# Windowed attention on 64 image passes: TensorE's round in another order, the output in a score bank, the normalised images held twice

## The chip, the cores and the metric

The kernel runs on one core of a Trainium2 chip. The metric is the device time of one execution in microseconds. Three runs of the kernel before took 764.14, 768.58 and 770.73 us, so the median is 768.58.

## What is computed

Two layers, each a group normalisation and a shifted-window attention with a residual, on 32 images of 16 x 16 tokens and 256 channels:

```python
x = x + _L0_conv_ref(_gn(x), ...)
x = x + _L1_conv_ref(_gn(x), ...)
# one layer, on windows of 64 tokens, 16 heads of 16 channels:
q, k, v = xw @ Wq.T, xw @ Wk.T, xw @ Wv.T + bv
qn, kn = q / norm(q), k / norm(k)
logits = einsum(qn, kn) * exp(min(logit_scale, LOG100)) + 16 * sigmoid(bias)
scores = softmax(where(mask, -inf, logits))
z = (scores @ v) @ Wo.T + bo
```

`_gn` takes mean and variance over a group of 8 channels and all tokens of an image.

## The kernel before

All images stay in SBUF (`x_all`). A **job** is one image in one layer; there are 64. Each engine runs the same function `iteration(j, base)` for rounds j = -3 to 67, unrolled at the ends and in loops of two rounds in between. In round j four jobs are in flight: `now` is job j, `before` j-1, `older` j-2 and `oldest` j-3; normalising works ahead for jobs j+1 to j+3. The order of the work on an engine is the order of the calls in its `iteration`, written out by hand; every engine goes through it strictly in that order, and they meet on semaphores.

TensorE, round j: the group sums of job j+2 (L433), q and k of `now` into both banks of `ps_qk` (L380, two halves of 6 matmuls), turning back the mixed values of `oldest` (L392), turning q and k of `before` into score banks 0 and 1 (L404), the output projection of `oldest` (L414 for the rounded part, L419 for the rest), the scores of `before` (L469), the mixing of `older`, that is probabilities times values (L486, L496), and v of `now` (L508). Matmuls with the weights take two parts of the operand, a rounded one and the rest, three products in all. The output projection writes `ps_mix` bank 0, as the mixing does; the mixing therefore waits until the residual of `oldest` has been added.

ScalarE: squares of q/k (L574), rounding the next normalised image (`round_xn`, L581), the rounded mixed values (L588), q masked by head (`keep_q`, L596), logarithm and exponential that seed the inverse roots (L609, L618), the exponential of the scores in two halves (L643), normalising job j+2 into the one buffer `xn32` (L626), and v (L651).

VectorE: group variance of job j+2 (four small operations, L803 to L809), moments of job j+3 (`moments`, L750), norm sums (L758, twice), the rest of the mixed values (L775), k (L767), residual (L794, twice), unit vectors of q/k (`make_unit`, L783, twice), and the division of the mixed values by their sums (`divide`, L816 to L823).

GpSimd: squares of the moments of job j+3 (`mean_squares`, L927 to L933), the rest of the next normalised image (`split_xn`, L919), Newton's step for the inverse roots (`newton`, L943 to L956), and the weighing of the probabilities of `before` with the bias (`weigh`, L963, four times).

So q/k of job j+1 in round j+1 waits for `split_xn` of round j (semaphore `xn_ready`), the unit vectors wait for `newton`, the mixing for the four weighings of the round before, the division for the mixing (`mix_done`), and `mean_squares` for `moments` (`bn_done`). A second pass with exact maxima stands behind a test at the end; it isn't taken with this input.

Of the kernel before, what the change touches and what calls it, by code (L numbers as in the profile page):

```python
# [83 lines left out]
def build(nc, x, weights, out, consts, table_scratch):  # L84
    with ExitStack() as ctx:
# [46 lines left out]
        xn32 = sb("xn32", [P, CC, TOKENS])  # L132
# [35 lines left out]
        z_cols = ps_mix[:, 0, :].rearrange("p (c t) -> p c t", c=CC)  # L168
# [177 lines left out]
        def _(pe):  # L346
# [60 lines left out]
            def project_out(t):  # L407
                if t is None:
                    return
                pe.wait_ge(mixed_hi, t.count(1, 1))  # L410
                for c in range(CC):
                    for a in range(2):
                        for part in range(2):
                            nc.tensor.matmul(z_cols[:, c, :], w_o[:, part, a, c * P:(c + 1) * P], mixed[:, 0, a, :],  # L414
                                             start=(c + a + part == 0), stop=False, skip_group_check=True)
                pe.wait_ge(mixed_ready, t.count(1, 1))
                for c in range(CC):
                    for a in range(2):
                        last = nc.tensor.matmul(z_cols[:, c, :], w_o[:, 0, a, c * P:(c + 1) * P], mixed[:, 1, a, :],  # L419
                                                start=False, stop=(a == 1), skip_group_check=True)  # L420
                last.then_inc(z_done, 1)
# [33 lines left out]
            def score(j, base, t):  # L455
# [5 lines left out]
                past(pe, exped, t.count(2, 0))  # L461
                refine(t)
# [14 lines left out]
            def mix(j, base, t):  # L477

                if t is None:
                    return  # L480
                past(pe, x_updated, t.count(2, 0))
                past(pe, mixed_ready, t.count(1, 0))
                pe.wait_ge(v_ready, t.count(1, 1))
                pe.wait_ge(weighted, t.count(4, 4))

                nc.tensor.matmul(mix_cols[:, 0, 0, :], probs[0:N, t.parity, 0, 0, 0, :, :].rearrange("p a n -> p (a n)"),  # L486
                                 v_ones[0:N, t.parity, 0, 0, 0, 0, :], start=True, stop=True, skip_group_check=True)
                for e in range(2):
                    for c in range(CC):
                        for r in range(GROUPS):  # L490
                            for a in range(2):
                                for w in range(2):
                                    if e + c + r + a + w == 0:
                                        continue
                                    at = slice(w * N, (w + 1) * N)
                                    last = nc.tensor.matmul(mix_cols[a * N:(a + 1) * N, w, (e * CC + c) * GROUPS + r, :], probs[at, t.parity, r, e, c, a, :],  # L496
                                                            v_ones[at, t.parity, e, c, r, a, :], start=True, stop=True, skip_group_check=True)
                last.then_inc(mix_done, 1)
# [13 lines left out]
            def iteration(j, base):  # L512
# [8 lines left out]
                sum_groups(j, base, job(j, base, 2))  # L521
                project_qk(now, 0)
                project_qk(now, 1)
                turn_back(oldest)
                turn(before)
                project_out(oldest)
                score(j, base, before)
# [6 lines left out]
                mix(j, base, older)  # L534
                if j == 0:
                    pe.wait_ge(w_split, split(0, base.exact, 1))
# [9 lines left out]
        def _(act):  # L546
# [29 lines left out]
            def round_xn(t):  # L576
# [4 lines left out]
                nc.scalar.activation(xn[:, 0, t.parity, :, :], xn32[:, :, :], ACT.Copy).then_inc(xn_hi, 1)  # L581
# [38 lines left out]
            def normalise(u):  # L620
# [3 lines left out]
                past(act, xn_ready, u.count(1, 0))  # L624
                for c in range(CC):
                    nc.scalar.activation(xn32[:, c, :], x_all[:, bass.ds(u.image, 1), c, :].rearrange("p o t -> p (o t)"), ACT.Identity,  # L626
# [27 lines left out]
            def iteration(j, base):  # L654
# [7 lines left out]
                round_xn(job(j, base, 1))  # L662
                square(now, 1)
                keep_mixed(oldest)
                keep_q(before, 0)
                keep_q(before, 1)
# [6 lines left out]

# [6 lines left out]
                if j == IMAGES + 2:  # L680
                    act.wait_ge(z_done, oldest.count(1, 1))
                    round_weights(1, 2)
                keep_shift(before)
                for i in range(GROUPS // 2):
                    exp(before, i)
                normalise(job(j, base, 2))
                keep_v(now)
                if j == -1:
                    round_weights(0, 1)
# [11 lines left out]
        def _(dve):  # L701
# [148 lines left out]
            def iteration(j, base):  # L850
# [5 lines left out]
                group_variance(j, base, after)  # L856
                moments(ahead)
# [9 lines left out]
                sum_norms(base, now, 0)  # L867
                sum_norms(base, now, 1)
# [6 lines left out]
                refine_shift(before)  # L875
                cap(before)
# [8 lines left out]
                divide(older)  # L885
                if j == 0 and not base.exact:
# [21 lines left out]
        def _(pool):  # L908
# [6 lines left out]
            def split_xn(t):  # L915
# [3 lines left out]
                nc.gpsimd.tensor_tensor(xn[:, 1, t.parity, :, :], xn32[:, :, :], xn[:, 0, t.parity, :, :], ALU.subtract).then_inc(xn_ready, 1)  # L919
# [45 lines left out]
            def iteration(j, base):  # L965
                if j >= 0:
                    mean_squares(job(j, base, WARM))
                split_xn(job(j, base, 1))
                newton(j, base)
                if j < 0:  # L970
                    mean_squares(job(j, base, WARM))
# [86 lines left out]
```

## Time and profile before

| | |
|---|---|
| runs, median | 768.58 us (764.14 to 770.73) |
| span of the profiled execution | 768.5 us; no time of its own is listed beside it |
| TensorE busy | 728.5 us, 95% |
| TensorE weight loads | 652.5 us, 85% |
| VectorE busy | 503.5 us, 66% |
| ScalarE busy | 498.5 us, 65% |
| GpSimd busy | 553.6 us, 72% |
| chain that ended last | TensorE 89% |
| DMA | in the first 80 us, then 19 to 32 GB/s for the stores and late loads |

The busy shares are means over the span. In a kernel with one loop the rows of the loop tell more: the timeline shows when each engine starts what, and in brackets how long it had been idle and who ended that. The chain of waits shows each piece of the path that ended last, with the time that it holds.

### The profile page before, as it was taken

To read this page: it belongs to the slowest core of one execution; us is meant where nothing else is said; L and a number is where in the kernel's file an instruction comes from. 1 tells how busy PE (TensorE), PEld (TensorE's weight loads), DVE (VectorE), ACT (ScalarE), POOL (GpSimd) and SP (SyncE) were. 2 spreads that over 40 slices of the span, in tenths; PEclk is the share of its full clock that TensorE was granted. 3 is DMA by queue.
4 is the path that set the end of the run, shared out by engine and by line. 5 is a ranking of instruction groups with operands and counts; after the bars stand their busy time and mean duration, and the time that the engine had idled before them with its cause. 6 is when DMAs were issued, how large, how long until landed. Compare 5 with 4: busy or idle time off the path is not lost.

```text
span 768.5 us, 38488 instructions
## 1 busy us (share of the span) xinstructions
PE 728.5 (95%) x15518; PEld 652.5 (85%) x15518; DVE 503.5 (66%) x1177; ACT 498.5 (65%) x848; POOL 553.6 (72%) x913
## 2 busy tenths in 40 slices
PE   3689899999999999999999999999999999999995
PEld 3578788888888889898989888888888888888984
DVE  4545466666666666667777667677766767776642
ACT  4556467676677667676777676666667666666650
POOL 4475668777877787788888777877777787777660
PEclk9789899999999999999999999999999999999995
DMA  4666200000000000000000000000000000000000
GB/s 116 156 157 172 65 0 0 0 1 0 0 0 0 0 0 0 0 0 0 1 0 0 28 28 14 27 27 25 16 27 27 14 27 27 27 14 27 29 31 32
DMA packets 14041, 21.45 MB, mean 28 GB/s; under 512 B 3756, under 2 KB 5045, under 8 KB 14005
## 3 DMA queue, kind: packets, MB, share of 16 engines
q1 hardware_dynamic: 13461, 20.23, 8.8%
q10 hardware_dynamic: 544, 0.79, 0.3%
q8 instruction: 17, 0.28, 0.2%
q14 instruction: 19, 0.16, 0.1%
HBM read 12.60 MB, written 8.42 MB: 27 GB/s over the span
## 4 chain that ended last, share of the span: by engine, by line
PE 89%; issue 3%; DVE 3%; DMA 2%; DVEq 1%; ACT 0%; SPq 0%; ACTq 0%
PE ps_qk L380 24%; PE ps_mix L496 17%; PE ps_qk L508 14%; PE ps_mix L414 9%; PE ps_score L404 7%; PE ps_score L469 6%; PE ps_mix L419 4%; PE ps_mix L392 4%; PE ps_mix L486 3%; DVE x_out L794 2%; DMA bias_rev<-table_scratch 1%; PE ps_score L433 1%; DMA table_scratch<-table 1%; DMA cpb<-in_L_cpb 0%; DVE exp_bias L737 0%
## 5 line engine op out<-in xcount | busy, mean ns | idle before, releaser
L963 POOL TENSOR_TENSOR probs<-probs,exp_bias 128x512 f32<-128x512 f32 x256 | 326.0, 1305 | 18.9 <-ACT probs L643 18.9
L380 PE MATMUL ps_qk<-w_qk,xn 128*128 128x512 f32 x768 | 200.0, 410 | 0.0
L643 ACT ACTIVATE probs<-ps_score,lower 128x1024 f32<-128x1024 f32 x128 | 135.7, 1111 | 66.8 <-PE ps_score L469 66.8
L380 PEld LDWEIGHTS ps_qk<-w_qk,xn 128*128 128x128 f32 x768 | 144.0, 194 | 30.2
L496 PE MATMUL ps_mix<-v_ones,probs 64*64 64x17 f32 x8064 | 133.4, 209 | 3.4 <-issue 3.4
L574 ACT ACTIVATE squares<-ps_qk 128x512 f32<-128x512 f32 x128 | 77.0, 602 | 87.1 <-PE ps_qk L380 87.1
L758 DVE TENSOR_REDUCE sums_sq<-squares 128x32 f32<-128x512 f32 x128 | 87.2, 682 | 68.9 <-ACT squares L574 68.8
L496 PEld LDWEIGHTS ps_mix<-v_ones,probs 64*64 64x64 f32 x8064 | 126.8, 136 | 5.5 <-issue 3.7
L783 DVE SCALAR_TENSOR_TENSOR unit<-root,ps_qk 128x512 f32<-128x512 f32 x128 | 82.4, 683 | 58.9 <-POOL root L953 58.9
L508 PE MATMUL ps_qk<-w_v,xn 128*128 128x256 f32 x768 | 113.9, 300 | 5.4 <-DVE unit L783 4.6
L508 PEld LDWEIGHTS ps_qk<-w_v,xn 128*128 128x128 f32 x768 | 100.2, 198 | 7.7 <-issue 6.0
L943 POOL TENSOR_TENSOR refined<-sums_sq,seed 128x66 f32<-128x66 f32 (+2 forms) x66 | 21.3, 322 | 97.6 <-ACT seed L618 97.5
L651 ACT ACTIVATE v_ones<-ps_qk 128x512 f32<-128x512 f32 x64 | 38.4, 601 | 77.4 <-PE ps_qk L508 77.4
L919 POOL TENSOR_TENSOR xn<-xn 128x512 fp32r<-128x512 f32 x64 | 82.0, 1281 | 5.5 <-ACT xn L581 5.5
L596 ACT ACTIVATE q_own<-ps_score,own_head 128x512 f32<-128x512 f32 x128 | 81.1, 693 | 0.0
L414 PE MATMUL ps_mix<-mixed,w_o 128*128 128x256 f32 x512 | 78.5, 296 | 1.4 <-ACT mixed L588 1.4
L469 PE MATMUL ps_score<-q_own,k_rows 32*64 32x128 f32 x4096 | 77.2, 278 | 2.4 <-DVE k_rows L767 1.2
L414 PEld LDWEIGHTS ps_mix<-mixed,w_o 128*128 128x128 f32 x512 | 65.0, 190 | 9.1 <-ACT mixed L588 2.0
L626 ACT ACTIVATE xn<-x_all,g_off,root 128x256 f32 (+1 forms) x128 | 69.5, 596 | 3.3 <-POOL g_off L956 3.3
L469 PEld LDWEIGHTS ps_score<-q_own,k_rows 32*64 32x64 f32 x4096 | 61.8, 130 | 11.2 <-ACT q_own L596 2.8
L404 PE MATMUL ps_score<-ident,unit 128*128 128x128 f32 x512 | 66.3, 273 | 0.0
L404 PEld LDWEIGHTS ps_score<-ident,unit 128*128 128x128 f32 x512 | 58.0, 140 | 0.3
(73 smaller groups left out, 867.8 us busy)
## 6 DMA issues: line engine op xcount, KB each, us to landing
x_all<-in_x SPq DMA_DIRECT2D x32, 256.0 KB, 3.1
out<-x_out SPq DMA_DIRECT2D x32, 256.0 KB, 2.1
bias_rev<-table_scratch SPq DMA_DIRECT2D x4, 452.0 KB
w_qk_in<-in_L_matrices ACTq DMA_DIRECT2D x1, 512.0 KB, 4.6
w_o_in<-in_L_matrices SPq DMA_DIRECT2D x4, 128.0 KB
w_qk_in<-in_L_matrices SPq DMA_DIRECT2D x1, 512.0 KB, 5.5
w_v_in<-in_L_matrices ACTq DMA_DIRECT2D x1, 256.0 KB, 4.9
w_v_in<-in_L_matrices SPq DMA_DIRECT2D x1, 256.0 KB, 6.2
```

Source lines behind the costliest of these rows:

```text
L380: last = nc.tensor.matmul(ps_qk[:, e, :], xn[:, px, t.parity, c, e * P:(e + 1) * P], w_qk[:, pw, c, :], start=(c == 0 and i == 0), stop=(c ...
L404: last = nc.tensor.transpose(to[:, e, c, :], unit[:, e, (n * CC + c) * P:(n * CC + c + 1) * P], ident[:, :])
L414: nc.tensor.matmul(z_cols[:, c, :], w_o[:, part, a, c * P:(c + 1) * P], mixed[:, 0, a, :], start=(c + a + part == 0), stop=False, skip_gro ...
L469: last = nc.tensor.matmul(ps_score[w * N:(w + 1) * N, r, cols:cols + 2 * N], k_rows[at, e, c, w * N:(w + 1) * N], q_own[at, e, c, w, :, :] ...
L496: last = nc.tensor.matmul(mix_cols[a * N:(a + 1) * N, w, (e * CC + c) * GROUPS + r, :], probs[at, t.parity, r, e, c, a, :], v_ones[at, t.p ...
L508: last = nc.tensor.matmul(v_cols[:, e, :], xn[:, px, t.parity, c, e * P:(e + 1) * P], w_v[:, pw, c, :], start=(c == 0 and i == 0), stop=(c ...
L596: nc.scalar.activation(q_own[:, :, :, :, a, :].rearrange("p e c w n -> p (e c w) n"), q_turned_to.rearrange("p e c (w n) -> p (e c w) n", ...
L643: nc.scalar.activation(probs[:, t.parity, 2 * i:2 * i + 2, :, :, :, :].rearrange("p r e c a n -> p r (e c a n)"), ps_score[:, 2 * i:2 * i ...
L758: nc.vector.tensor_reduce(sums_sq[:, e * NORMS:(e + 1) * NORMS], squares[:, e, :].rearrange("p (h d) -> p h d", d=HD), AX_X, ALU.add).then ...
L783: nc.vector.scalar_tensor_tensor(out=unit[:, e, :].rearrange("p (h d) -> p h d", d=HD), in0=by, scalar=INV_NORM_TOP, in1=ps_qk[:, e, :].re ...
L919: nc.gpsimd.tensor_tensor(xn[:, 1, t.parity, :, :], xn32[:, :, :], xn[:, 0, t.parity, :, :], ALU.subtract).then_inc(xn_ready, 1)
L963: nc.gpsimd.tensor_tensor(pr, pr, exp_bias[:, t.layer, r, :, :, :, :].rearrange("p e c a n -> p (e c a n)"), ALU.mult).then_inc(weighted, 1)
```

## The change

On TensorE the group sums go behind q/k, the scores behind the mixing, and the output projection writes score bank 3 in place of the mixing's bank 0. It waits for the exponentials of job j-2 before it writes there; the waits of the mixing (v and the weighings) now stand in the middle of the output projection, and the scores wait for the residual. The mixing's first double-width matmul goes. `xn32` is held twice, by parity. ScalarE rounds and normalises ahead of the exponentials, does logarithm and seed ahead of q, and keeps v between the two exponentials. On VectorE the group variance goes between the two norm sums and the moments behind the division. On GpSimd Newton's step and the squares of the moments come first, then the split.

```diff
-        xn32 = sb("xn32", [P, CC, TOKENS])
+        xn32 = sb("xn32", [P, 2, CC, TOKENS])
...
-        z_cols = ps_mix[:, 0, :].rearrange("p (c t) -> p c t", c=CC)
+        z_cols = ps_score[:, 3, :].rearrange("p (c t) -> p c t", c=CC)
...
+            def await_mix(t):
+                pe.wait_ge(v_ready, t.count(1, 1))
+                pe.wait_ge(weighted, t.count(4, 4))
+
+            def project_out(t, older):
                 if t is None:
                     return
+                if older is not None:
+                    pe.wait_ge(exped, older.count(2, 2))
                 pe.wait_ge(mixed_hi, t.count(1, 1))
...
                 pe.wait_ge(mixed_ready, t.count(1, 1))
+                if older is not None:
+                    await_mix(older)
...
                 past(pe, exped, t.count(2, 0))
+                oldest = job(j, base, -3)
+                if oldest is not None:
+                    pe.wait_ge(x_updated, oldest.count(2, 2))
                 refine(t)
...
-                past(pe, x_updated, t.count(2, 0))
-                past(pe, mixed_ready, t.count(1, 0))
-                pe.wait_ge(v_ready, t.count(1, 1))
-                pe.wait_ge(weighted, t.count(4, 4))
-
-                nc.tensor.matmul(mix_cols[:, 0, 0, :], probs[0:N, t.parity, 0, 0, 0, :, :].rearrange("p a n -> p (a n)"),
-                                 v_ones[0:N, t.parity, 0, 0, 0, 0, :], start=True, stop=True, skip_group_check=True)
+                if job(j, base, -3) is None:
+                    await_mix(t)
...
-                                    if e + c + r + a + w == 0:
-                                        continue
...
-                sum_groups(j, base, job(j, base, 2))
                 project_qk(now, 0)
                 project_qk(now, 1)
+                sum_groups(j, base, job(j, base, 2))
                 turn_back(oldest)
                 turn(before)
-                project_out(oldest)
-                score(j, base, before)
+                project_out(oldest, older)
...
                 mix(j, base, older)
+                score(j, base, before)
...
-                past(act, xn_ready, u.count(1, 0))
+                past(act, xn_ready, u.count(1, -1))
                 for c in range(CC):
-                    nc.scalar.activation(xn32[:, c, :], x_all[:, bass.ds(u.image, 1), c, :].rearrange("p o t -> p (o t)"), ACT.Identity,
+                    nc.scalar.activation(xn32[:, u.parity, c, :], x_all[:, bass.ds(u.image, 1), c, :].rearrange("p o t -> p (o t)"), ACT.Identity,
...
                 square(now, 0)
-                round_xn(job(j, base, 1))
                 square(now, 1)
                 keep_mixed(oldest)
-                keep_q(before, 0)
-                keep_q(before, 1)
...
+                keep_q(before, 0)
+                keep_q(before, 1)
+                round_xn(job(j, base, 1))
+                normalise(job(j, base, 2))
                 keep_shift(before)
-                for i in range(GROUPS // 2):
-                    exp(before, i)
-                normalise(job(j, base, 2))
+                exp(before, 0)
                 keep_v(now)
+                exp(before, 1)
...
-                group_variance(j, base, after)
-                moments(ahead)
+                if j < 0:
+                    group_variance(j, base, after)
+                    moments(ahead)
...
                 sum_norms(base, now, 0)
+                if j >= 0:
+                    group_variance(j, base, after)
                 sum_norms(base, now, 1)
...
                 make_unit(base, now, 0)
                 divide(older)
+                if j >= 0:
+                    moments(ahead)
...
             def iteration(j, base):
-                if j >= 0:
-                    mean_squares(job(j, base, WARM))
+                newton(j, base)
+                mean_squares(job(j, base, WARM))
                 split_xn(job(j, base, 1))
-                newton(j, base)
-                if j < 0:
-                    mean_squares(job(j, base, WARM))
```

TensorE, round 3 as it was (names are the destination and the operands):

```order
L433 MATMUL ps_score<-bn_sum,consts 128x4
L380 MATMUL ps_qk<-w_qk,xn 128x512 x12
L392 MATMUL ps_mix<-ident,o_rows 128x2x64 x4
L404 MATMUL ps_score<-ident,unit 128x128 x8
L414 MATMUL ps_mix<-mixed,w_o 128x256 x8
L419 MATMUL ps_mix<-mixed,w_o 128x256 x4
L469 MATMUL ps_score<-q_own,k_rows 64x128 x32
L486 MATMUL ps_mix<-v_ones,probs 128x17
L496 MATMUL ps_mix<-v_ones,probs 64x17 x63
L508 MATMUL ps_qk<-w_v,xn 128x256 x12
```

And the same round of the change:

```order
L380 MATMUL ps_qk<-w_qk,xn 128x512 x12
L441 MATMUL ps_score<-bn_sum,consts 128x4
L392 MATMUL ps_mix<-ident,o_rows 128x2x64 x4
L404 MATMUL ps_score<-ident,unit 128x128 x8
L420 MATMUL ps_score<-mixed,w_o 128x256 x8
L427 MATMUL ps_score<-mixed,w_o 128x256 x4
L500 MATMUL ps_mix<-v_ones,probs 64x17 x64
L480 MATMUL ps_score<-q_own,k_rows 64x128 x32
L512 MATMUL ps_qk<-w_v,xn 128x256 x12
```

The scores stand behind the mixing, and the output's destination is `ps_score`.

VectorE at the end of a round in the loop, before, with what each row waits for: division, then the next round's group variance.

```order
L816 TENSOR_SCALAR sums<-ps_mix 128x32 [waits mix_done]
L209 ISA
L818 TENSOR_TENSOR least<-least,ps_mix 128x32 [waits sum_step]
L819 REGISTER_ALU
L820 RECIPROCAL inv_sums<-sums 128x32 [waits sum_step]
L821 REGISTER_ALU
L823 TENSOR_TENSOR o_rows<-ps_mix,inv_sums 128x512 [waits turned_back,sum_step]
L801 REGISTER_ALU
L803 TENSOR_SCALAR neg_mean<-ps_score 128x2 [waits gn_offset,group_summed]
```

The same place in the change:

```order
L819 TENSOR_SCALAR sums<-ps_mix 128x32 [waits mix_done]
L209 ISA
L821 TENSOR_TENSOR least<-least,ps_mix 128x32 [waits sum_step]
L822 REGISTER_ALU
L823 RECIPROCAL inv_sums<-sums 128x32 [waits sum_step]
L824 REGISTER_ALU
L826 TENSOR_TENSOR o_rows<-ps_mix,inv_sums 128x512 [waits turned_back,sum_step]
L748 ISA
L753 ISA [waits moment_step,x_moved1]
L753 BN_STATS bn<-x_all 128x6
```

The moments (`BN_STATS`) now follow the division, whose first row waits for the mixing of the same round.

GpSimd at the start of a round in the loop, before: squares, split, then Newton's step.

```order
L927 TENSOR_TENSOR mean_sq<-bn 128x4 [waits bn_done]
L928 TENSOR_SCALAR bn<-bn 128x4
L929 ISA
L930 TENSOR_TENSOR bn<-bn,mean_sq 128x4 [waits moment_step]
L931 REGISTER_ALU
L209 REGISTER_ALU [waits moment_step]
L933 TENSOR_TENSOR bn_sum<-bn 128x4 [waits group_summed]
L918 ISA
L919 TENSOR_TENSOR xn<-xn 128x512 [waits xn_hi]
L942 REGISTER_ALU
L943 TENSOR_TENSOR refined<-sums_sq,seed 128x66 [waits seeded]
```

And in the change, from the last row of Newton's step on:

```order
L964 TENSOR_TENSOR g_off<-root,neg_mean 128x2 [waits newton_step]
L934 REGISTER_ALU
L935 TENSOR_TENSOR mean_sq<-bn 128x4 [waits bn_done]
L936 TENSOR_SCALAR bn<-bn 128x4
L937 ISA
L938 TENSOR_TENSOR bn<-bn,mean_sq 128x4 [waits moment_step]
L939 REGISTER_ALU
L209 REGISTER_ALU [waits moment_step]
L941 TENSOR_TENSOR bn_sum<-bn 128x4 [waits group_summed]
L926 REGISTER_ALU
L927 TENSOR_TENSOR xn<-xn 128x512 [waits xn_hi]
```

The split (`xn<-xn`) stands directly behind the squares in both; the squares have moved behind Newton's step, and what they wait for, `bn_done`, now comes from the end of VectorE's round.

## Rows read from the trace of the kernel before

**Rows 1.** Busy time by stretches: us, busy (instructions) per engine, granted clock, DMA share, GB/s

```profile
300.00:400.00 100.00, 99.69 (x2185) 89.41 (x2184) 74.19 (x170) 70.93 (x121) 81.89 (x127) 1.00 0.00 0
```

**Rows 2.** Timeline of TensorE, starts of q/k: start, us, what

```profile
16.94 4.53 PE L380 MATMUL ps_qk<-w_qk,xn 128*128 128x512 f32 x12
...
107.84 2.35 PE L380 MATMUL ps_qk<-w_qk,xn 128*128 128x512 f32 x9
...
729.73 2.95 PE L380 MATMUL ps_qk<-w_qk,xn 128*128 128x512 f32 x12
```

**Rows 3.** Chain of waits, one round: start, us held, what

```profile
406.71 2.90 PE ps_qk L380 x12
...
412.46 1.14 PE ps_score L469 x63
...
413.60 0.39 PE ps_mix L486 x2
...
415.97 1.62 PE ps_qk L508 x12
```

**Rows 4.** Waits in total: us, times, longest

```profile
PEld ps_mix L486 <- issue: 20.0, 59, 0.5
...
PE ps_mix L486 <- DVE x_out L794: 3.9, 13, 1.0
```

**Rows 5.** Timeline of a steady round, all engines

```profile
405.03 0.19 DVE L816 TENSOR_SCALAR sums<-ps_mix 128x32 f32<-128x32 f32 x1 [0.52 <-PE ps_mix L496]
...
405.64 0.69 DVE L823 TENSOR_TENSOR o_rows<-ps_mix,inv_sums 128x512 f32<-128x512 f32 x1
...
406.43 0.28 PE L433 MATMUL ps_score<-bn_sum,consts 128*128 128x4 f32 x2
...
406.56 3.04 PE L380 MATMUL ps_qk<-w_qk,xn 128*128 128x512 f32 x12
...
406.74 0.16 DVE L803 TENSOR_SCALAR neg_mean<-ps_score 128x2 f32<-128x2 f32 x1 [0.41 <-PE ps_score L433]
...
407.68 0.74 DVE L750 BATCH_NORM_STATS2 bn<-x_all 128x6 f32<-128x256 f32 x2
...
409.64 0.60 ACT L574 ACTIVATE squares<-ps_qk 128x512 f32<-128x512 f32 x1 [0.28 <-PE ps_qk L380]
```

**Rows 6.** Timeline of the first rounds, VectorE and GpSimd

```profile
4.10 0.75 DVE L750 BATCH_NORM_STATS2 bn<-x_all 128x6 f32<-128x256 f32 x2 [4.10 <-DMA x_all<-in_x]
...
4.93 0.20 POOL L927 TENSOR_TENSOR mean_sq<-bn 128x4 f32<-128x4 f32 x1 [2.77 <-DVE bn L750]
...
22.13 0.69 DVE L758 TENSOR_REDUCE sums_sq<-squares 128x32 f32<-128x512 f32 x1 [0.94 <-ACT squares L574]
...
25.23 1.28 DVE L783 SCALAR_TENSOR_TENSOR unit<-root,ps_qk 128x512 f32<-128x512 f32 x2 [2.41 <-POOL root L953]
```

**Rows 7.** Timeline of GpSimd in a steady round

```profile
182.62 5.03 POOL L963 TENSOR_TENSOR probs<-probs,exp_bias 128x512 f32<-128x512 f32 x4 [0.20 <-ACT probs L643]
...
187.61 0.20 POOL L927 TENSOR_TENSOR mean_sq<-bn 128x4 f32<-128x4 f32 x1
...
188.59 1.27 POOL L919 TENSOR_TENSOR xn<-xn 128x512 fp32r<-128x512 f32 x1
```

**Rows 8.** Timeline of TensorE in early rounds, with its idle time before

```profile
51.74 0.54 PE L496 MATMUL ps_mix<-v_ones,probs 64*64 64x17 f32 x25 [0.98 <-issue]
...
64.03 0.42 PE L496 MATMUL ps_mix<-v_ones,probs 64*64 64x17 f32 x14 [1.04 <-issue]
...
64.37 2.77 PE L508 MATMUL ps_qk<-w_v,xn 128*128 128x256 f32 x12
...
92.43 2.50 PE L508 MATMUL ps_qk<-w_v,xn 128*128 128x256 f32 x10 [0.76 <-issue]
...
95.01 4.72 PE L380 MATMUL ps_qk<-w_qk,xn 128*128 128x512 f32 x12
```

**Rows 9.** Busy time by stretches, an early one

```profile
65.00:70.00 5.00, 5.00 (x24) 4.50 (x23) 2.17 (x8) 1.25 (x3) 2.75 (x6) 0.70 0.60 161
```

More of the change, by code:

```diff
@@ L405, in turn @@
                     last.then_inc(done, 1)
-            def project_out(t):
+            def await_mix(t):
+                pe.wait_ge(v_ready, t.count(1, 1))
+                pe.wait_ge(weighted, t.count(4, 4))
+            def project_out(t, older):
                 if t is None:
                     return
+                if older is not None:
+                    pe.wait_ge(exped, older.count(2, 2))
                 pe.wait_ge(mixed_hi, t.count(1, 1))
@@ L580, in round_xn @@
                 past(act, v_done, t.count(1, -1))
-                nc.scalar.activation(xn[:, 0, t.parity, :, :], xn32[:, :, :], ACT.Copy).then_inc(xn_hi, 1)
+                nc.scalar.activation(xn[:, 0, t.parity, :, :], xn32[:, t.parity, :, :], ACT.Copy).then_inc(xn_hi, 1)
             def keep_mixed(t):
@@ L874, in iteration @@
                 add_residual(oldest, 1)
-                refine_shift(before)
-                cap(before)
                 if j == IMAGES:
@@ L885, in iteration @@
                 divide(older)
+                if j >= 0:
+                    moments(ahead)
+                refine_shift(before)
+                cap(before)
                 if j == 0 and not base.exact:
@@ L918, in split_xn @@
                 pool.wait_ge(xn_hi, t.count(1, 1))
-                nc.gpsimd.tensor_tensor(xn[:, 1, t.parity, :, :], xn32[:, :, :], xn[:, 0, t.parity, :, :], ALU.subtract).then_inc(xn_ready, 1)
+                nc.gpsimd.tensor_tensor(xn[:, 1, t.parity, :, :], xn32[:, t.parity, :, :], xn[:, 0, t.parity, :, :], ALU.subtract).then_inc(xn_ready, 1)
             def mean_squares(u):
```

## The prediction

> **What bounds the kernel now.** I read the busy time by stretches first. In the middle of the run TensorE is busy for 99.7 of 100 us at the full granted clock of 1.00 (2.4 GHz), the other three engines for 71 to 82 [rows 1]. So the loop is TensorE's own work, and there is no stall in it to take away beyond splinters. The timeline of TensorE gives the length of a round, from one start of the q/k projection to the next: 107.84 to 729.73 us for 56 rounds, 11.1 us each. The first seven rounds, 16.94 to 107.84, took 90.9 us, 13.0 each [rows 2]. The chain of waits shows one round as TensorE spends it [rows 3]. The splinters are in front of the mixing: its first weight load waits for the issue of its waits, 20.0 us in 59 rounds, and for the residual that still reads the mixing's bank, 3.9 us in 13 [rows 4]. Those are what TensorE itself can win.
>
> The question is then whether the other engines' new order still lets TensorE run without a stall. For that I follow everything that a round must finish before the next q/k projection may start.
>
> **The change on TensorE.** The output goes into bank 3 of the scores, so the mixing no longer waits for the residual, and its waits are issued ahead of the last four output matmuls, behind work that is in the queue. The first double-width matmul of the mixing, 0.39 us with its stall, becomes two of the small ones, of which the other 126 records fill 413.99 to 415.97, 1.98 us [rows 3]: 0.03. Taken with [rows 4] this is at best 24 us over the run, 0.35 to 0.4 us a round. The score now waits for the residual and for q and k, but the mixing (2.0 us) lies between the turning and it, so I cost these waits at nothing; without that cover the score would stall by the residual's 0.9 us. The group sums behind q/k cost their 0.12 us in either place.
>
> **The change on VectorE and GpSimd.** Here is the step that decides. Before, the moments of the image three ahead are taken at the start of VectorE's round, beside the q/k projection, and GpSimd squares them right after the weighing of the round before. Now VectorE takes them **behind the division**, which is the last thing that it does in a round, and GpSimd, which is in order, has their squares **ahead of the split of the next image**. The next q/k projection waits for that split. So the end of each round now hangs on the division. The cycle, counted from the start of q/k in round j:
>
> - q/k takes 2.90 us on TensorE [rows 3], then come the group sums. VectorE starts the group variance 0.31 us after they do (406.43 to 406.74) and needs 0.94 us for it (406.74 to 407.68) [rows 5]: 2.90 + 0.31 + 0.94 = 4.15 us. The second half's squares are there by 3.1 + 0.6 = 3.7 us (409.64 against 406.56, the start of that q/k) [rows 5], so the second norm sum now starts at 4.15, 0.4 later than its data allow.
> - From the start of that sum to the start of the unit vectors, through the logarithm, the seed and Newton's four steps, a round in which nothing else stood in between took 25.23 - 22.13 = 3.10 us [rows 6]: 7.25. In today's steady rounds ScalarE copies q between sum and logarithm; the change moves that behind the seed, so I take the clean round. The two unit products take 1.28 [rows 6]: 8.53.
> - The mixing is through at 415.97 - 406.71 - 1.14 (the score, now behind it) + 0.13 (the sums, now ahead) - 0.36 (the first matmul) = 7.9 us. The unit vectors are the later of the two releases by 0.6.
> - The division takes 405.03 to 406.33, 1.30 us [rows 5]: 9.83. The moments take 0.75 and reach GpSimd 0.08 us after their end (4.85 to 4.93) [rows 6]: 10.66. Squares and sums take 187.61 to 188.59, 0.98, and the split 1.27 [rows 7]: 12.91. For the hop from GpSimd to TensorE I take 0.1, the size of the one that the rows show.
>
> The cycle is **13.0 us**, against the 10.75 of TensorE's work. It replaces the 11.1 us of today: +1.9 us a round. Are the other cycles shorter? With the mixing in place of the unit vectors it is 12.4. Through the weighing (5.03 us [rows 7]): hop 0.1, last output 0.5, mixing 2.0, division 1.3, moments and hop 0.83, squares 0.98, split 1.27, weighing 5.03, 12.0 us. Both give way. GpSimd ends the weighing 5.0 us after q/k starts, when the seed comes at about 5.6, so it isn't late for Newton. The second copy of the normalised images frees ScalarE from waiting for the split, and costs nothing; normalising has more than 2 us ahead of the exponential.
>
> How many rounds: the moments exist up to round 60, so the start of q/k is held back up to round 61. From round 7 to 61 that is 54 intervals, 54 x 1.9 = 103 us. The first seven rounds are as long as the new cycle already; some of their stalls are TensorE's instruction issue in the mixing, which is 0.6 us off the cycle, so I add 3 us (0 to 10). The last rounds gain under 1. With the clock untouched: 768.5 + 103 + 3 = **874 us**. The span of the profiled execution, 768.5, lies on the median of the runs, 768.58, so no correction.
>
> **The clock.** With a round of 13.0 and 10.75 of work, TensorE stands idle for about 2.3 us in each round, between v and q/k. No steady round has such a gap now, and what the clock does after one must be read at the start of the run. There TensorE stood still for 0.98 us at 50.8, for 1.04 at 63.0 and for 0.76 at 91.7. After the first nothing happened; after the second v took 2.77 us in place of 1.62 and the granted clock of 65 to 70 us was 0.70 [rows 9]; after the third ten of the twelve matmuls of v took 2.50 and q/k 4.72 in place of 2.90 [rows 8]. That is the lower level, 1.2 GHz, over one or two products. So two of three shorter gaps than the new one brought a fall, 1.1 us of it where it lay on v and 1.8 on q/k. The new gap is right ahead of q/k, which is the head of the cycle, so a fall is paid in full. But dense products stand on both sides of it, where the mixing's small matmuls stood beside the old ones, so I take half of the 57 rounds held back, at 1.6 us: 57 x 0.5 x 1.6 = 46 us. Bounds: none, and 1.8 in all 57, 103 us.
>
> The Trainium skill (TensorE: Matmul & The Clock Gate, section "Why this matters for your kernels") warns of throughput drops only for idle gaps that are longer than this one. By it the clock would stay up and the time would be 874 us; the early rounds here speak against it, with falls after 1.04 and 0.76 us.
>
> Sum: 874 + 46 = **920 us**.
>
> **The rivals.**
> - *The clock stays at 2.4 GHz*: the cycle of 13.0 alone, 874 us. For it: the fall that did not come after 0.98 us, and the dense products on both sides. Against: the gap is twice as long as those that brought a fall. 0.26.
> - *Faster, TensorE stays the bound*: if a round's moments didn't hold back the split, the cycle would end at the weighing and be under 10.75, and TensorE would win its splinters: 768.5 - 24 = 745 us. It decides at a cycle of 10.75 us, 2.25 below my sum. Each term has its own row, and the order of VectorE and GpSimd is fixed by the program, so for this the hops or the overlaps would have to be misread by 2 us. 0.04.
> - *The cycle is real but shorter*, 11.5 to 12.5 us, because the steps overlap more than their rows show: 785 to 850 us. 0.04.
> - *The clock falls in nearly every round*, or for longer than q/k, so that turning and output are slow too: 960 to 1000 us. 0.06.
> - *Nothing moves*: the wait sits on GpSimd, which is idle for a fifth of the time, and TensorE doesn't feel it. It would need a split that is a round early, which the order excludes. 0.02.
>
> My forecast has 0.58. One per cent, some 8 us, is about what a measurement of this kernel can tell from no change. Faster 0.04, within 1% 0.02, slower 0.94. The range takes in the case with the clock up, less a little for a cycle of 12.8 us, and ends where the falls come in nine rounds of ten: 864 to 958.
>
> **What would show it.** GpSimd's squares of the moments wait for VectorE's moments some 3 us in each of about 60 rounds, near 190 us, where its largest wait on that pair is now small. TensorE's first q/k matmul waits for GpSimd's split, 2 us or more in each round, over 100 us in all, in a place that has no wait now. The start of q/k comes every 13.0 us in rounds without a fall, and the mixing's first matmul has no issue gap left. VectorE has the group variance between its two norm sums. TensorE's busy share falls below 86%, and the granted clock shows slices below 9 through the whole loop; if these stay at 9, the first rival holds. Starts of q/k every 10.8 us would prove the whole sum wrong; the first place to look would then be GpSimd's queue, whether the split waits behind the squares at all.

## The result and the profile after

The changed kernel takes **949.08 us** (948.28 to 956.52) against 769.12 for the kernel before, measured beside each other: a ratio of 1.237 [1.230, 1.244]. The prediction was 920 us, in a range of 864 to 958. Time and sign are right; two of its terms are off, one by 51 us and one by 35, in opposite directions, and the experiments are mostly about these. Two executions that have no trace stand out: the one of 956.52 us shows a mean granted clock of 0.741, where the other three of the changed kernel have 0.946 to 0.950, and one of experiment 8 took 1784.54 us, about twice its others, for a reason that is not known, and is left out there.

The page of the changed kernel: busy time, the granted clock in 40 slices, and the chain that ended last by engine and by line.

```profile
PE 756.3 (80%) x15518; PEld 658.4 (69%) x15518; DVE 509.7 (54%) x1177; ACT 517.6 (55%) x848; POOL 552.4 (58%) x913
...
PEclk9789999899899999998989999899999999999995
...
POOL 42%; issue 34%; PE 10%; DMA 4%; DVE 4%; POOLq 2%; SPq 2%; ACT 1%; DVEq 0%
...
POOL probs L971 26%; PE ps_qk L380 4%; DMA x_all<-in_x 4%; POOL xn L927 4%; POOL refined L955 2%; POOL refined L953 2%; POOL refined L951 2%; POOL root L961 2%; POOL mean_sq L935 2%; POOL bn L938 1%; PE ps_mix L500 1%; POOL bn L936 1%; POOL g_off L964 1%; PE ps_score L427 1%; PE ps_score L420 1%
```

TensorE's share went from 95% to 80%. The clock has slices below 9 in the loop, where it was 1.00 [rows 1], but few. The chain now names GpSimd first, its weighing above all. That line is a trap, as the fourth experiment shows.

The starts of q/k on TensorE, to be read against [rows 2]:

```profile
17.28 5.46 PE L380 MATMUL ps_qk<-w_qk,xn 128*128 128x512 f32 x12 [6.20 <-POOL xn L927]
...
116.39 3.05 PE L380 MATMUL ps_qk<-w_qk,xn 128*128 128x512 f32 x12 [2.27 <-POOL xn L927]
...
881.42 3.05 PE L380 MATMUL ps_qk<-w_qk,xn 128*128 128x512 f32 x12 [1.65 <-POOL xn L927]
...
903.39 2.96 PE L380 MATMUL ps_qk<-w_qk,xn 128*128 128x512 f32 x12
```

From round 7 to round 61 it is 881.42 - 116.39 = 765.0 us, 14.17 a round, where the kernel before took 600.4, 11.12. That is 164.6 of the 179.1 us by which the span grew (947.6 against 768.5). The first seven rounds give 8.5, the last ones 6. In the last ones the output projection waits for the weighings, with nothing else to do; two such waits are in the timeline, 2.6 us together, and the other 3.4 are not split up here:

```profile
918.80 0.71 PE L427 MATMUL ps_score<-mixed,w_o 128*128 128x256 f32 x4 [1.08 <-POOL probs L971]
...
931.16 1.19 PE L427 MATMUL ps_score<-mixed,w_o 128*128 128x256 f32 x4 [1.49 <-POOL probs L971]
```

One steady round of the changed kernel, all engines, with the idle time in brackets:

```profile
144.11 5.01 POOL L971 TENSOR_TENSOR probs<-probs,exp_bias 128x512 f32<-128x512 f32 x4
...
144.28 3.05 PE L380 MATMUL ps_qk<-w_qk,xn 128*128 128x512 f32 x12 [2.24 <-POOL xn L927]
...
147.49 0.16 DVE L806 TENSOR_SCALAR neg_mean<-ps_score 128x2 f32<-128x2 f32 x1 [0.20 <-PE ps_score L441]
...
148.07 1.08 DVE L812 TENSOR_SCALAR sums_sq<-g_var 128x2 f32<-128x2 f32 x1
...
149.06 0.68 DVE L761 TENSOR_REDUCE sums_sq<-squares 128x32 f32<-128x512 f32 x1
...
152.53 1.29 DVE L786 SCALAR_TENSOR_TENSOR unit<-root,ps_qk 128x512 f32<-128x512 f32 x2 [0.30 <-POOL root L961]
...
153.73 0.18 DVE L819 TENSOR_SCALAR sums<-ps_mix 128x32 f32<-128x32 f32 x1
...
154.94 0.74 DVE L753 BATCH_NORM_STATS2 bn<-x_all 128x6 f32 x2
...
155.76 0.20 POOL L935 TENSOR_TENSOR mean_sq<-bn 128x4 f32<-128x4 f32 x1 [3.00 <-DVE bn L753]
...
156.76 1.26 POOL L927 TENSOR_TENSOR xn<-xn 128x512 fp32r<-128x512 f32 x1
...
157.98 1.29 POOL L971 TENSOR_TENSOR probs<-probs,exp_bias 128x512 f32<-128x512 f32 x1
```

Read it from 144.28. The variance (L806) starts 3.21 us later, as reckoned from [rows 5]. Its last step (L812) takes 1.08 us, and ends as the fourth weighing of the block of 144.11 ends (144.11 + 5.01 = 149.12). The second norm sum starts at 4.78, the units (L786) at 8.25, the division at 9.45, the moments at 10.66, GpSimd's squares (L935) at 11.48, the split at 12.48, and q/k of the next round with the next block at about 13.88. The waits in total:

```profile
POOL mean_sq L935 <- DVE bn L753: 187.7, 62, 4.1
...
PE ps_qk L380 <- POOL xn L927: 136.6, 61, 6.2
...
PE ps_score L427 <- DVE mixed L778: 23.4, 41, 0.7
```

The first two are what the prediction said would be seen, 188 us and 137 us. The third is new.

### The profile page after: what moved, and what is told of

Read it like the earlier page. It is cut to its first block, busy times and chain, and to the rows that moved or that the text cites. A ratio compares the mean times of both kernels' runs of the same rounds, so it can differ in the third digit from the quotient of the medians.

```text
span 947.6 us, 38578 instructions
## 1 busy us (share of the span) xinstructions
PE 756.3 (80%) x15518; PEld 658.4 (69%) x15518; DVE 509.7 (54%) x1177; ACT 517.6 (55%) x848; POOL 552.4 (58%) x913
## 4 chain that ended last, share of the span: by engine, by line
POOL 42%; issue 34%; PE 10%; DMA 4%; DVE 4%; POOLq 2%; SPq 2%; ACT 1%; DVEq 0%
POOL probs L971 26%; PE ps_qk L380 4%; DMA x_all<-in_x 4%; POOL xn L927 4%; POOL refined L955 2%; POOL refined L953 2%; POOL refined L951 2%; POOL root L961 2%; POOL mean_sq L935 2%; POOL bn L938 1%; PE ps_mix L500 1%; POOL bn L936 1%; POOL g_off L964 1%; PE ps_score L427 1%; PE ps_score L420 1%
## 5 line engine op out<-in xcount | busy, mean ns | idle before, releaser
L380 PE MATMUL ps_qk<-w_qk,xn 128*128 128x512 f32 x768 | 226.6, 451 | 138.7 <-POOL xn L927 136.6
L971 POOL TENSOR_TENSOR probs<-probs,exp_bias 128x512 f32<-128x512 f32 x256 | 321.0, 1286 | 15.0 <-ACT probs L647 15.0
L380 PEld LDWEIGHTS ps_qk<-w_qk,xn 128*128 128x128 f32 x768 | 160.8, 216 | 187.2 <-issue 145.6
L647 ACT ACTIVATE probs<-ps_score,lower 128x1024 f32<-128x1024 f32 x128 | 142.3, 1113 | 40.9 <-PE ps_score L480 40.9
L935 POOL TENSOR_TENSOR mean_sq<-bn 128x4 f32<-128x4 f32 x64 | 16.5, 257 | 187.7 <-DVE bn L753 187.7
L512 PE MATMUL ps_qk<-w_v,xn 128*128 128x256 f32 x768 | 109.4, 292 | 5.6 <-DVE unit L786 4.6
L512 PEld LDWEIGHTS ps_qk<-w_v,xn 128*128 128x128 f32 x768 | 96.1, 191 | 16.6 <-issue 16.4
L786 DVE SCALAR_TENSOR_TENSOR unit<-root,ps_qk 128x512 f32<-128x512 f32 x128 | 82.4, 684 | 18.4 <-POOL root L961 18.1
L420 PE MATMUL ps_score<-mixed,w_o 128*128 128x256 f32 x512 | 77.8, 295 | 3.7 <-ACT mixed L592 3.7
L420 PEld LDWEIGHTS ps_score<-mixed,w_o 128*128 128x128 f32 x512 | 66.1, 192 | 13.7 <-issue 5.0
L427 PE MATMUL ps_score<-mixed,w_o 128*128 128x256 f32 x256 | 46.0, 303 | 25.9 <-DVE mixed L778 23.4
```

What stands on the lines that cost most here:

```text
L380: last = nc.tensor.matmul(ps_qk[:, e, :], xn[:, px, t.parity, c, e * P:(e + 1) * P], w_qk[:, pw, c, :], start=(c == 0 and i == 0), stop=(c ...
L512: last = nc.tensor.matmul(v_cols[:, e, :], xn[:, px, t.parity, c, e * P:(e + 1) * P], w_v[:, pw, c, :], start=(c == 0 and i == 0), stop=(c ...
L647: nc.scalar.activation(probs[:, t.parity, 2 * i:2 * i + 2, :, :, :, :].rearrange("p r e c a n -> p r (e c a n)"), ps_score[:, 2 * i:2 * i ...
L786: nc.vector.scalar_tensor_tensor(out=unit[:, e, :].rearrange("p (h d) -> p h d", d=HD), in0=by, scalar=INV_NORM_TOP, in1=ps_qk[:, e, :].re ...
L971: nc.gpsimd.tensor_tensor(pr, pr, exp_bias[:, t.layer, r, :, :, :, :].rearrange("p e c a n -> p (e c a n)"), ALU.mult).then_inc(weighted, 1)
```

## The experiments

Each was timed beside the kernel before, which took 768.3 to 770.7 us in these comparisons.

**1. Moments back at the start of VectorE's round**, all else as changed.

```diff
                 if j < 0:
                     group_variance(j, base, after)
-                    moments(ahead)
+                moments(ahead)
...
                 divide(older)
-                if j >= 0:
-                    moments(ahead)
```

> The changed kernel, with the moments of job j+3 back at the start of VectorE's round; all else as changed. Theory 1 (the moments behind the division close a cycle of 14.0 us over weighing, variance, norm sum, Newton, units, division, moments, squares and split): the cycle is cut, what is left is GpSimd's own loop, weighing 5.0 + norm sum to the end of Newton 3.8 + squares 1.0 + split 1.26 = 11.1 us a round, or TensorE's 10.75: 750 to 775 us. Rival (the loss lies in TensorE's new order and the waits in the middle of the output projection): the time stays over 900 us.

Measured: 793.39 us, ratio 1.032 [1.028, 1.035]. One call in another place takes away 156 of the 180 us. Rounds take 11.5 us. TensorE is the bound but for one stall, which is in the timeline of this kernel:

```profile
312.42 0.63 PE L392 MATMUL ps_mix<-ident,o_rows 128*128 128x128 f32 x4
...
313.18 1.14 DVE L812 TENSOR_SCALAR sums_sq<-g_var 128x2 f32<-128x2 f32 x1
...
314.82 0.67 DVE L778 TENSOR_TENSOR mixed<-ps_mix,mixed 128x512 fp32r<-128x512 f32 x1
...
315.63 0.74 PE L427 MATMUL ps_score<-mixed,w_o 128*128 128x256 f32 x4 [0.61 <-DVE mixed L778]
```

The rest of the mixed values (L778) comes behind the second norm sum, that behind the step L812, which takes 1.14 us; the last output matmuls (L427) come 0.61 us after they could. So the loss is not in TensorE's order. The time missed the expected 750 to 775; that the stall is the reason is what experiment 5 shows.

**2. The group variance in PSUM**, moments late.

```diff
+        g_var_ps = ps_score[:, 2, 2 * CC:3 * CC]
...
-                nc.vector.scalar_tensor_tensor(out=g_var[:, :], ...
+                nc.vector.scalar_tensor_tensor(out=g_var_ps, ...
-                nc.vector.tensor_scalar(sums_sq[:, 2 * NORMS:], g_var[:, :], EPS_GN, 4.0, ALU.max, ALU.mult)
+                nc.vector.tensor_scalar(sums_sq[:, 2 * NORMS:], g_var_ps, EPS_GN, 4.0, ALU.max, ALU.mult)
```

> The changed kernel, with the group variance kept in PSUM, so that its last step has no tensor in SBUF to read; same values. Theory 1a (that step, 1.07 us in place of 0.28, is held by GpSimd's running weighing): the step takes under 0.3 us, the second norm sum starts 0.75 us earlier, 54 rounds x 0.75 = 40 us less: about 910 us. Rival (the step is long for another reason, or another path of the round is as long): no change, 945 to 950 us.

Measured: 917.11 us, ratio 1.192 [1.188, 1.196], 32 us less. The step in the groups by line, of the kernel before:

```profile
L809 DVE TENSOR_SCALAR sums_sq<-g_var 128x2 f32<-128x2 f32 x64 | 30.1, 471 | 2.2
```

of the changed kernel:

```profile
L812 DVE TENSOR_SCALAR sums_sq<-g_var 128x2 f32<-128x2 f32 x64 | 47.7, 746 | 2.7 <-DVE g_var L810 0.3
```

and of this one:

```profile
L813 DVE TENSOR_SCALAR sums_sq<-ps_score 128x2 f32<-128x2 f32 x64 | 10.2, 159 | 2.5 <-DVE ps_score L811 0.3
```

A step on 128 x 2 elements takes 0.16 us when it reads PSUM, and 0.17 to 1.08 when it reads SBUF, and when it is long it ends with GpSimd's running operation: it is held. This holds without exception: in the changed kernel 41 of the 64 steps take over 0.3 us, each ends 0.02 to 0.03 us after a weighing ends, and none of the 23 short ones has a GpSimd operation running on beside it. With the input in PSUM 42 of the 64 steps run beside a weighing, in 0.16 us. Rounds without a fall of the clock went from 13.88 and 14.02 to 13.06 and 13.22: the 13.0 of the prediction. The Trainium skill (GPSIMD Engine Reference, section "8. Key points") says that GpSimd shares its SBUF interfaces with VectorE, and that VectorE's instructions in a 2-port mode or with two SBUF inputs contend with it. The trace agrees that the two engines contend. The held step has one SBUF input, and no trace shows whether it runs in such a mode. The second case, two SBUF inputs, is in the trace with the roles turned round: in a round of the changed kernel in which VectorE multiplies two SBUF tensors (L740), GpSimd's 128 x 4 square takes 0.92 us in place of 0.20 and ends with the multiplication:

```profile
424.76 1.06 DVE L740 TENSOR_TENSOR exp_bias<-bias_rev,masks 128x512 f32<-128x512 f32 x1
...
424.92 0.92 POOL L935 TENSOR_TENSOR mean_sq<-bn 128x4 f32<-128x4 f32 x1 [3.00 <-DVE bn L753]
```

**3. TensorE kept busy in its gap**, by nine 128x128 matmuls on constants behind v.

```diff
                 project_v(now)
+                if now is not None and older is not None:
+                    pe.wait_ge(o_ready, older.count(1, 1))
+                    for _ in range(9):
+                        nc.tensor.matmul(ps_mix[:, 0, 320:448], ident[:, :], group_mean[:, :], ...)
```

> The changed kernel, with nine extra 128x128 matmuls on constants behind v, into columns that nothing reads, so that TensorE is busy for about 1.9 us of its 2.3 us gap. Theory (falls of the clock come in pairs in 16 of 54 rounds and cost 0.65 us each): the granted clock stays at 1.00 and 10 us go, 939 us. Rival (falls cost what the prediction took, or work hidden beside them): 905 to 925 us. If the extra work itself is in the way: over 950 us.

Measured: 944.16 us, ratio 1.226 [1.222, 1.231]. The falls in the loop are gone and the 54 rounds take 754.4 us in place of 765.0. The extra work costs some 5 us outside of them. So the clock was worth 10.6 us, over 17 stretches at the lower level: 0.6 each. Why so little, the changed kernel shows in a round with a fall:

```profile
172.65 4.60 PE L380 MATMUL ps_qk<-w_qk,xn 128*128 128x512 f32 x12 [2.00 <-POOL xn L927]
...
178.15 0.69 DVE L761 TENSOR_REDUCE sums_sq<-squares 128x32 f32<-128x512 f32 x1
```

and the clock beside it:

```profile
173.20:176.70 3.50, 3.50 (x10) 2.70 (x9) 0.69 (x1) 0.60 (x1) 3.50 (x4) 0.52 0.00 0
...
176.70:186.90 10.20, 8.33 (x233) 7.60 (x231) 6.53 (x17) 7.38 (x12) 4.05 (x11) 1.00 0.00 0
```

q/k takes 4.60 us, 1.55 more. But the norm sum starts at 178.15 - 172.65 = 5.50, only 0.72 later than in a round without: the weighing is over by then, so that L812 isn't held (0.17 us). The hold had already taken the time that the fall takes.

**4. The split ahead of the squares** on GpSimd, moments late.

```diff
                 newton(j, base)
-                mean_squares(job(j, base, WARM))
                 split_xn(job(j, base, 1))
+                mean_squares(job(j, base, WARM))
```

> The changed kernel, with GpSimd's split of the next image ahead of the squares of the moments. Theory 1 (the cycle runs through the weighing, which is behind both): the split leaves the cycle, 14.0 - 1.26 = 12.7 us a round, 949 - 68 = 880 us, and TensorE's wait for the split is gone. Rival (the cycle is the one of the prediction, through q/k, which needs the split to be late): it is open now, the round falls to the next bound, 11 us, and the time to about 775 us.

Measured: 793.84 us, ratio 1.032 [1.028, 1.036]. My theory 1, which I had taken from the chain of waits after the result, fell; the prediction's own cycle stood. Its timeline:

```profile
308.72 2.97 PE L380 MATMUL ps_qk<-w_qk,xn 128*128 128x512 f32 x12
...
308.76 0.20 POOL L935 TENSOR_TENSOR mean_sq<-bn 128x4 f32<-128x4 f32 x1 [1.86 <-DVE bn L753]
...
309.74 5.00 POOL L971 TENSOR_TENSOR probs<-probs,exp_bias 128x512 f32<-128x512 f32 x4
...
312.43 1.10 DVE L812 TENSOR_SCALAR sums_sq<-g_var 128x2 f32<-128x2 f32 x1
```

q/k starts at 308.72, before the squares (308.76) are even begun. The moments are as late as they were, the weighing is behind them, and rounds take 11.5. L812 is still held, here to the end of the third of the four weighings (309.74 + 3.75 = 313.49, and L812 ends at 312.43 + 1.10 = 313.53). What closed the cycle is the split behind the squares.

The weighing's large share of the chain does not come from the hold either: in the second experiment, in which nothing is held, it is 27%, and in this one, with the cycle open, 32%. The chain walks back along GpSimd's own queue and puts down GpSimd's wait for the moments as "issue", as in these pieces of the second experiment's chain:

```profile
230.88 2.97 issue
...
233.89 0.19 POOL mean_sq L936
```

The waits of the same kernel name VectorE's moments for this time, 188.0 us in 62 waits. So the chain never leaves GpSimd there, and its shares say what GpSimd did, not what set the round. In this kernel one round, the one at the change of layer, shows the lower clock and takes 15.6 us; all others take 11.0 to 11.7.

**5. Moments early and variance in PSUM**: 1 and 2 together.

> Moments early (as in the first experiment) and group variance in PSUM (as in the second). Theory (with the moments early TensorE is the bound again, and its only stall, 0.6 to 0.75 us before the last output matmuls, comes from the norm sum that stands behind the held step of the variance): the stall goes, a round is TensorE's own 10.75 us, 793 - 56 x 0.75 = 751 us, under the kernel before. Rival (another wait takes the stall's place, the weighings that the output projection now waits for): 775 us or more.

Measured: **744.92 us**, ratio 0.967 [0.965, 0.970]: faster than both kernels. The middle of its run:

```profile
300.00:400.00 100.00, 99.69 (x2374) 90.24 (x2378) 74.62 (x178) 75.57 (x127) 81.97 (x136) 1.00 0.00 0
```

TensorE is busy as in [rows 1] and does more in it. The chain of one round, start and time held:

```profile
305.78 2.81 PE ps_qk L381 x12
...
311.25 0.51 PE ps_score L428 x4
...
311.75 1.99 PE ps_mix L501 x128
...
314.88 1.62 PE ps_qk L513 x12
...
316.50 2.79 PE ps_qk L381 x12
```

No stall is left before the last output matmuls or the mixing, and a round takes 10.58 to 10.72 us, where 11.12 were taken before: 56 x 0.47 = 26 us. This is what all the rest of the change is worth together: the orders of TensorE and ScalarE, the score bank, the hoisted waits and the second copy. The variance in PSUM is in it too; it moves nothing in the kernel before (10), and here it takes the stall away.

**6. Variance in PSUM and the extra matmuls**, moments late: 2 and 3 together.

> The second experiment (variance in PSUM, moments late) with the nine extra matmuls behind v. Theory (without the hold of the weighing the cycle runs through q/k itself, so that a fall of the clock is paid in full, about 1.5 us each for 19 of them, where it was 0.65): the extra matmuls keep the clock up and take 28 us, 917 to 889 us. Rival (a fall costs the same with and without the hold, 0.65 us): 905 us or more.

Measured: 899.80 us, ratio 1.169 [1.164, 1.173], 17 us under the second. The 54 rounds take 710.4 us in place of 735.8, 25.4 less for 17 low stretches, 1.5 each; the extra work gives 8 back in the first and last rounds. Two rounds of the second experiment, one with a fall, one without, show that it is now paid in full (q/k and the norm sum):

```profile
221.65 4.60 PE L381 MATMUL ps_qk<-w_qk,xn 128*128 128x512 f32 x12 [2.25 <-POOL xn L928]
...
227.16 0.69 DVE L762 TENSOR_REDUCE sums_sq<-squares 128x32 f32<-128x512 f32 x1
...
236.27 3.06 PE L381 MATMUL ps_qk<-w_qk,xn 128*128 128x512 f32 x12 [2.23 <-POOL xn L928]
...
240.24 0.69 DVE L762 TENSOR_REDUCE sums_sq<-squares 128x32 f32<-128x512 f32 x1
```

5.51 against 3.97 us from q/k to the norm sum: 1.54, where it was 0.72 with the hold. This is also why the second experiment won 29 us in its 54 rounds (765.0 - 735.8) and not 54 x 0.8 = 43. The expected 889 us left out the 8 that the extra work costs.

**7. The kernel before with the late moments alone**, and GpSimd's order that they need.

```diff
                 group_variance(j, base, after)
-                moments(ahead)
+                if j < 0:
+                    moments(ahead)
...
                 divide(older)
+                if j >= 0:
+                    moments(ahead)
... (GpSimd)
-                if j >= 0:
-                    mean_squares(job(j, base, WARM))
-                split_xn(job(j, base, 1))
                 newton(j, base)
-                if j < 0:
-                    mean_squares(job(j, base, WARM))
+                mean_squares(job(j, base, WARM))
+                split_xn(job(j, base, 1))
```

> The kernel before with one part of the change alone: VectorE's moments behind the division, and GpSimd with Newton's step, squares, split in this order. Theory (this part alone carries the loss): q/k 2.9, turning and output 2.9, score 1.1, mixing 2.4, division 1.2, moments 0.8, squares 1.0, split 1.4 make 13.8 us a round in TensorE's old order: 768 + 54 x 2.7 + 8 = 920 us, with some falls of the clock up to 935. Rival (TensorE's order, the bank or ScalarE's order carry a third or more of it): under 880 us.

Measured: 1055.05 us, ratio 1.371 [1.366, 1.376]. This part alone carries more than the whole loss; the rest of the change wins some 106 us of it back. Its size was off by 135 us: expected were 920. Rounds without a fall take 14.22 to 14.33 us, most take 15.3 to 16.9. ScalarE's largest wait, for the split, as it has one copy of the normalised image, is large too:

```profile
ACT xn L626 <- POOL xn L922: 306.8, 62, 8.7
```

Two candidates for the excess, hence the next ones.

**9. The same with two copies.** In the seventh, `xn32` held by parity as in the change.

> The seventh experiment (kernel before, moments late) with the normalised images held twice, as in the change. Theory (ScalarE's 307 us of waiting for the split are off the path but for the second half of q/k, which waits 0.3 us for v behind it): 54 x 0.3 = 16 us less, about 1037 us, and most of the excess over 920 stays, since it lies in falls of the clock. Rival (the single copy is what made the seventh so much slower than reckoned): under 980 us.

Measured: 1050.95 us, ratio 1.363 [1.356, 1.370]. ScalarE's wait for the split is gone, and the time is 4 us less, within the noise of the two: the 307 us of waiting were off the path, nearly all. The expected 1037 was missed by 14 us. Here 53 of the 54 rounds have a fall of the clock, so that there is hardly a round without one to compare.

**11. The seventh with seven extra matmuls** behind v.

> The seventh experiment (kernel before, moments late) with seven extra matmuls behind v, 1.5 us of the gap that it has there before the group sums. Theory (its rounds without a fall take 14.25 us, the others 15.3 to 16.9, since the clock falls in most rounds): with the clock kept up all rounds take 14.3, 54 x 1.4 = 75 us less, about 975 us. Rival (the longer rounds come from something else): 1040 us or more.

Measured: 970.59 us, ratio 1.264 [1.257, 1.271], 84 us under the seventh. A stretch of 100 us of the seventh:

```profile
400.00:500.00 100.00, 83.90 (x1651) 72.17 (x1633) 49.58 (x118) 48.20 (x80) 53.46 (x89) 0.86 0.00 0
```

and of this one:

```profile
400.00:500.00 100.00, 91.13 (x1701) 79.38 (x1694) 53.95 (x127) 51.66 (x88) 59.72 (x94) 0.97 0.00 0
```

So in TensorE's old order the same late moments cost 84 us through the clock, where they cost 11 in the new. There the group sums, which wait for the squares, stand alone between v and q/k. Nearly all rounds of the loop take 14.2 to 14.5 now; the longer ones, up to 16.5, are at the change of layer. Against the 920 expected of the seventh, 14.3 in place of 13.8 is 27 us; most of the rest is in the first and last rounds. With the clock held up in both orders, 970.59 here against 944.16 in the third, TensorE's order and the rest of the change are worth 26 us, as in the fifth.

**8. The fifth with the output in the mixing's bank**, as before the change, with the mixing's wait for the residual and its old first matmul.

> The fifth experiment with the output back in the mixing's bank, the wait of the mixing for the residual, and its double-width first matmul. In this order the mixing stands right behind the output. Theory (the score bank is what makes this order possible): each mixing waits for the residual, 0.4 us to its start and 0.9 for it, 56 x 1.3 = 73 us more than the fifth: about 824 us. Rival (the residual is hidden, the bank gives nothing): as the fifth, about 751 us.

Measured: 904.87 us (three executions), ratio 1.177 [1.171, 1.183], 81 us over the expected 824. Rounds without a fall take 11.95, 1.3 more than in the fifth, as expected. But 42 of 56 rounds have a fall, and most of these take 13.5 to 13.7: some 68 us. The first and last rounds hold most of the rest. The values of v (L518) after a fall, the stall of the next mixing, and v without one:

```profile
242.91 2.68 PE L518 MATMUL ps_qk<-w_v,xn 128*128 128x256 f32 x12
...
252.54 0.39 PE L496 MATMUL ps_mix<-v_ones,probs 64*128 64x17 f32 x2 [1.09 <-DVE x_all L803]
...
255.97 1.69 PE L518 MATMUL ps_qk<-w_v,xn 128*128 128x256 f32 x12
```

A stall of 1.0 us ahead of the mixing is followed by a fall in most rounds; with one of 2.2 us between v and q/k it was 17 of 54. What decides is not isolated here: the two kernels differ in more than the place of the stall.

**10. The kernel before with the variance in PSUM.**

> The kernel before with the group variance kept in PSUM, and nothing else. Theory (there the step falls mostly between the weighings, 0.28 us, and TensorE is the bound): no change, 765 to 773 us. Rival (the hold, 0.47 us in the mean, is on the path there too): 56 x 0.3 = 17 us less, 753 us.

Measured: 769.71 us, ratio 1.000 [0.998, 1.003]. The step went from 0.47 to 0.16 us and nothing else moved: off the path, the hold is free.

## Why the prediction was right, and where it wasn't

- **What bounds the kernel, and the cycle.** Right. Moments, squares, split and q/k close a cycle across the rounds, and 1 and 4 cut it at two different links with the same result, 793 and 794 us. In 4 the moments stay late, so their lateness costs only through the split.
- **The cycle's 13.0 us.** Mis-sized: measured 13.88 and 14.02 in rounds without a fall. By the steps of the prediction: the variance 4.15 became 4.78, since its last step is held by the weighing (0.63); the 3.10 us from norm sum to units, from an unrolled round, are 3.47 in the loop (0.37 more: 0.16 of it ahead of Newton's last step, 0.13 ahead of the logarithm); the division, the moments, the squares and the split came out within 0.1 us. The hint stood in the groups by line of the kernel before (row in experiment 2): a mean of 0.47 us for an operation on two columns. 54 x 0.95 = 51 us. With the hold taken away (2) the rounds are at 13.06 and 13.22.
- **The clock's 46 us.** Mis-sized the other way: 10.6 us. A fall came in 17 of 54 rounds, not in half, and cost 0.6 us, not 1.6, as the hold hid it. In 6, without the hold, one costs 1.5 us, so the price that the early rounds gave was right for the path that I had drawn. One error hid the other, by luck: had I seen the hold, and kept the clock's term, the sum would have been 971 us, outside the range. The prediction also misread how often a fall comes. It counts falls after two of three early stalls of the kernel before; that trace has two more: 1.19 us up to 47.62, with the granted clock at 1.00 from 47.7 to 51.7, and 1.38 us up to 78.39, with the granted clock at 0.50 from 78.3 to 81.6:

```profile
78.39 0.41 PE L496 MATMUL ps_mix<-v_ones,probs 64*64 64x17 f32 x7 [1.38 <-issue]
```

So a fall came in three of five, after 0.76, 1.04 and 1.38 us, and not after 0.98 and 1.19: the length of a stall alone didn't tell.
- **The rule on idle gaps** of the Trainium skill (TensorE: Matmul & The Clock Gate, section "Why this matters for your kernels"), which would have let the clock stay up: the traces disagree. It fell after gaps of 2.2 us here, and after 1.0 in 8.
- **TensorE's own gain**, at best 24 us: right in size, 26 us in 5, and lost here beneath the cycle.
- **The rivals.** "The clock stays up", 874: the clock did nearly stay up, and the time was 949, by the hold. "TensorE stays the bound", 745: its condition didn't hold, but its number is that of 5, where it does. There was no term for the last rounds' 6 us, and the first seven gave 8.5 us where 3 were taken (0 to 10). By terms: 920 + 51 - 35 + 5.5 + 6 = 947.5, against a span of 947.6.

## What to carry to other kernels

Before work is moved to the end of a round on one engine, follow it through the queues of the others to what the next round starts with: an order that is harmless inside a round can close a cycle over the round's edge, and that cycle's length is the new round. A line with a large share in the chain of waits need not be in the cycle, as the weighing wasn't; cutting two links shows which one holds. A stall is to be priced with what it does to the clock and with what hides it, and both depend on what stands beside it.

## What the runs showed of the hardware

- A VectorE operation on 2 columns of SBUF took 0.17 us alone and up to 1.08 (1.33 in the kernel before) beside GpSimd's two-input operations, to whose end it was held every time; with its input in PSUM it took 0.16 (2, 5, 10). GpSimd's 0.20 us became 0.92 beside a two-input one of VectorE.
- How often the clock fell did not follow the length of the gap: 2.2 us between the products of v and q/k, 17 of 54 rounds; 1.0 us between output and mixing, 42 of 56 (8); 1.6 and 0.9 us ahead of and behind the group sums, between v and q/k, 51 of 54 (7). No run isolates what decides. Extra matmuls in the gap, of no use otherwise, won 84 us in one kernel (11), 17 in another (6) and 5 in the changed one (3).
